# Layer norm behind attention on VectorE: three runs of four tiles, or eight steps of one or two tiles between the bias steps

## The chip, the cores and the metric

The kernel runs on one core of a Trainium2 chip. The metric is the device time of one execution in microseconds (us), the median of several runs.

## The reference

The whole program is one transformer block: adaptive layer norm, attention with a relative bias, a gated residual, a second adaptive layer norm, and a mixture of eight experts (top 2) with a gated residual. There are 8 batches of 512 tokens, 256 channels and 16 heads of width 16.

```python
mod = (_silu(L0_c) @ L0_wmod).reshape(L0_c.shape[0], 6, 1, -1)
sa, ca, ga, sb, cb, gb = ...
h = _layernorm(x, axis=-1) * (1 + ca) + sa
x = x + ga * _L0_attn_ref(h, W_qkv, b_qkv, W_out, b_out, rel_bias)
h = _layernorm(x, axis=-1) * (1 + cb) + sb      # the layer norm of this study
x = x + gb * _L0_ffn_ref(h, gate_w, expert_bias, w_up, w_down)
```

The second layer norm takes the mean and the variance of each token's 256 channels of the gated attention result, subtracts the mean, divides by the root of the variance plus 1e-5, and scales and shifts by rows of the batch.

## The kernel before

**Stages.** Four parts follow one another: preparation, attention (from about 88 us to 845 us of the profiled execution), routing, and experts. Only attention is touched.

**Attention.** An outer loop goes over the 8 batches, an inner one over the 16 heads n of a batch. The first and the last batch are written out, the six between them are one loop body (`Fori`). All engines run their own instruction streams, in the order of the code, and meet at semaphores. One head is one step. TensorE (PE) makes the scores of 4 tiles of 128 queries by 512 keys (L888, two buffers in PSUM), turns the exponentials of the head before, in two pairs of tiles (L897), and weighs the values of the head before that (L912). VectorE (DVE) adds the bias to each score tile and takes its minimum (`add_bias`, L761, four a step, t from 0 to 3), and moves the first pair of turned tiles out of PSUM (`evacuate`, L769). ScalarE (ACT) takes the exponentials (L683) and moves the second pair (L690). The tile t of `sn` is written again one head later, when its exponential is taken.

**The shared bank.** One PSUM bank, `ps_m`, serves in turn for the small products of a batch: the table `USES` gives each its step. Those of the steps 9, 10, 12 and 13 project q1, k1, v0 and v1 for the next batch ("project steps"; some 1.9 us of PE); "back1" at step 11 turns one group of outputs back, which VectorE divides (L783, L785); VectorE adds the bias of v (`values`, L776) behind v0 and v1.

**The layer norm.** During batch b the results of batch b-1 are finished. On VectorE, `between(b, n, kind)` is called twice a step: with n between bias tile 1 and `evacuate`, and with n + 0.5 between bias tile 3 and bias tile 0 of the next step. At 9.5 stands `moments` (four BN_STATS, L806, then four BN_AGGR, L812), at 10.5 `centre` (four SCALAR_TENSOR_TENSOR, L819: minus the mean, times the scale row), at 12.5 `normal` (four of the same kind, L828: times 1/deviation, plus the shift row). Each works on tiles of 128x256 in SBUF.

**GpSimd (POOL)** runs, in this order, in the middle of a batch: the split of q1 into bf16 parts (`split`: L417, L419, L423, L425), `deviation` (L618, L620; waits for `mv_done`, all four BN_AGGR), `split_piece` 2 of the experts' weights (L578, L580), the split of k1 (the same four lines), `split_piece` 3, `move_v` (L568, waits for `values` of v1), and `rest_of` (L606, L610; waits for `h2_done`, all four of `normal`). In the last batch there is nothing to project or to split of q and k.

**Behind it.** PE turns the normalised rows (L959) at the steps 14 and 14.5, after `h2_done`. SyncE stores them, and loads the stacks of q and k for the next batch (L445) when the last scores are made.

Of the kernel before, what the change touches and what calls it, by code (L numbers as in the profile page):

```python
# [16 lines left out]
B, S, D = 8, 512, 256  # L17
# [5 lines left out]
TB = S // P  # L23
# [16 lines left out]
def at_least(engine, semaphore, value):  # L40

    if not isinstance(value, int) or value > 0:
        engine.wait_ge(semaphore, value)


def apart(engine, passed):

    engine.sem_inc(passed, 1)
# [259 lines left out]
        (15.5, "logits"))  # L308
FROM_BEFORE = ("back3", "turn0", "turn1", "out0", "out1", "rows0", "rows1", "logits")
FOR_NEXT = ("q0", "k0", "q1", "k1", "v0", "v1")  # L310
MOMENTS, CENTRED, NORMAL = 9.5, 10.5, 12.5


def attention(nc, ahead, logits, x, h1t, mod_rows, ext_rows, splits, w_up_t, w_down_t, w_parts, rest_rows, h2_rows, sums):
# [10 lines left out]
    with ExitStack() as ctx:  # L325
# [59 lines left out]
        def uses_of(kind):  # L385

            return [(n, u) for n, u in USES
                    if not (kind == "first" and u in FROM_BEFORE) and not (kind == "last" and u in FOR_NEXT)]
# [5 lines left out]
        def use(b, kind, name):  # L394

            return uses_before(b, kind) + [u for _, u in uses_of(kind)].index(name)

        def end_use(name):

            return uses_before(B - 1, "last") + len(uses_of("last")) + FROM_BEFORE.index(name)  # L400
# [344 lines left out]
        def _(dve):  # L745
# [25 lines left out]
            def values(b, j, at):  # L771

                dve.wait_ge(used, at + 1)

                at_least(dve, v_moved, b * 2)
                dve.tensor_tensor(v_next[:, 2 * j:2 * j + 2, :], ps_m[:, :].rearrange("p (t n) -> p t n", n=D),  # L776
                                  b_v[:, :].unsqueeze(1).to_broadcast([P, 2, D]), ALU.add).then_inc(freed, 1)

            def back(b, g, at):

                dve.wait_ge(used, at + 1)
                turned_back = ps_m[:, :].rearrange("p (h t w) -> p h t w", h=TB, t=TB)
                dve.reciprocal(inv[:, :, :], turned_back[:, :, :, DK]).then_inc(inv_done, 1)  # L783
                dve.wait_ge(inv_done, b * GROUPS + g + 1)
                dve.tensor_tensor(on[:, :, g * TB * DK:(g + 1) * TB * DK].rearrange("p t (h d) -> p h t d", d=DK),  # L785
                                  turned_back[:, :, :, 0:DK], inv[:, :, :].unsqueeze(3).to_broadcast([P, TB, TB, DK]),
                                  ALU.mult).then_inc(freed, 1)

            def gate_out(b, j, at):

                dve.wait_ge(used, at + 1)
                dve.wait_ge(x_in, b * 48 + 48)

                at_least(dve, rest_out, b * 16)
                dve.wait_ge(sums_zeroed, 16 * (B + 1))
                dve.tensor_tensor(gated[:, 2 * j:2 * j + 2, :], ps_m[:, :].rearrange("p (t n) -> p t n", n=D),
                                  ga[:, :].unsqueeze(1).to_broadcast([P, 2, D]), ALU.mult).then_inc(freed, 1)

                dve.wait_ge(freed, at + 1)
                dve.sem_inc(gated_done, 1)  # L800

            def moments(b):

                dve.wait_ge(x1_done, b * 2 + 2)
                for t in range(TB):
                    dve.bn_stats(stats[:, t, :], gated[:, t, :]).then_inc(stats_done, 1)  # L806

                at_least(dve, rstd_done, b)
                dve.wait_ge(stats_done, (b + 1) * TB)
                apart(dve, dve_passed)  # L810
                for t in range(TB):
                    dve.bn_aggr(mv[:, t, :], stats[:, t, :]).then_inc(mv_done, 1)  # L812

            def centre(b):

                dve.wait_ge(mv_done, (b + 1) * TB)
                apart(dve, dve_passed)
                for t in range(TB):
                    dve.scalar_tensor_tensor(out=xb[:, t, :], in0=gated[:, t, :], scalar=mv[:, t, 0:1], in1=mod2[:, D:2 * D],  # L819
                                             op0=ALU.subtract, op1=ALU.mult).then_inc(centred, 1)  # L820

            def normal(b):

                dve.wait_ge(rstd_done, b + 1)
                dve.wait_ge(centred, (b + 1) * TB)
                apart(dve, dve_passed)
                for t in range(TB):
                    dve.scalar_tensor_tensor(out=xb[:, t, :], in0=xb[:, t, :], scalar=rstd[:, t:t + 1], in1=mod2[:, 0:D],  # L828
                                             op0=ALU.mult, op1=ALU.add).then_inc(h2_done, 1)

            def keep_logits(b, at):
                dve.wait_ge(used, at + 1)
                dve.tensor_copy(logits[:, bass.ds(b * TB, TB), :],
                                ps_m[:, 0:TB * NE].rearrange("p (t e) -> p t e", e=NE)).then_inc(freed, 1)

            def between(b, n, kind):
                for m, u in uses_of(kind):
                    if m == n and u == "back3":
                        back(b - 1, 3, use(b, kind, u))
                    elif m == n and u[:4] == "back":  # L840
                        back(b, int(u[4]), use(b, kind, u))
                    elif m == n and u[:3] == "out":
                        gate_out(b - 1, int(u[3]), use(b, kind, u))
                    elif m == n and u[0] == "v":
                        values(b + 1, int(u[1]), use(b, kind, u))
                    elif m == n and u == "logits":
                        keep_logits(b - 1, use(b, kind, u))
                if kind != "first" and n == MOMENTS:
                    moments(b - 1)
                if kind != "first" and n == CENTRED:  # L850
                    centre(b - 1)
                if kind != "first" and n == NORMAL:
                    normal(b - 1)

            for j in range(2):
                values(0, j, 4 + j)
# [1 line left out]
            def batch(b, kind):  # L858
                for n in range(NH):
                    if kind == "first" and n % TB == 0:  # L860
                        dve.wait_ge(ahead.loaded[n // TB], 16 * TB)
                    add_bias(b, n, 0)
                    add_bias(b, n, 1)
                    between(b, n, kind)
                    if kind != "first" or n > 0:
                        evacuate(b * NH + n - 1, (n + 1) % 2)
                    add_bias(b, n, 2)
                    add_bias(b, n, 3)
                    between(b, n + 0.5, kind)
# [3 lines left out]
            back(B - 1, 3, end_use("back3"))  # L873
            for j in range(2):
                gate_out(B - 1, j, end_use(f"out{j}"))
            moments(B - 1)
            centre(B - 1)
            normal(B - 1)
            keep_logits(B - 1, end_use("logits"))

        @block.tensor
# [823 lines left out]
```

## Time and profile before

| | us |
|---|---|
| median of 3 runs | 1387.36 (1382.64 to 1391.23) |
| profiled execution, its own time | 1386.03 |
| its span, first to last instruction | 1384.4 |
| busy in the span: PE / DVE / ACT / POOL | 1148.3 / 918.4 / 670.2 / 693.5 |

The profiled execution is 1.33 us below the median and 1.63 us above its own span. The busy times are sums over stages with different limits, so they say little about one step of attention; for that the rows below show the instructions in order of time. A start of the copy L769 marks the same point of each step, and the distance between two of them is the length of a step.

### The profile page before, as it was taken

To read this page: it belongs to the slowest core of one execution; us is meant where nothing else is said; L and a number is where in the kernel's file an instruction comes from. 1 tells how busy PE (TensorE), PEld (TensorE's weight loads), DVE (VectorE), ACT (ScalarE), POOL (GpSimd) and SP (SyncE) were. 2 spreads that over 40 slices of the span, in tenths; PEclk is the share of its full clock that TensorE was granted. 3 is DMA by queue.
4 is the path that set the end of the run, shared out by engine and by line. 5 is a ranking of instruction groups with operands and counts; after the bars stand their busy time and mean duration, and the time that the engine had idled before them with its cause. 6 is when DMAs were issued, how large, how long until landed. Compare 5 with 4: busy or idle time off the path is not lost. (4 is left out here: it accounts for less than half of the span.)

```text
span 1384.4 us, 33297 instructions
## 1 busy us (share of the span) xinstructions
PE 1148.3 (83%) x11290; PEld 898.9 (65%) x11291; DVE 918.4 (66%) x2185; ACT 670.2 (48%) x1038; POOL 693.5 (50%) x715
## 2 busy tenths in 40 slices
PE   5469999898998998998999861399999999999910
PEld 3236776676766766766777541288888888888810
DVE  4547888687786885885888846655555555555556
ACT  4248776675765766765768630222222222222212
POOL 3215155354551543463433332857666766666656
PEclk9779999999898998998999995599999999999965
DMA  9596853663556356526636117114342443442354
GB/s 308 182 208 185 238 165 92 151 130 95 152 104 146 124 110 144 119 81 151 130 79 163 47 52 262 47 38 109 47 109 44 112 106 61 95 106 46 46 153 129
DMA packets 123137, 168.47 MB, mean 122 GB/s; under 512 B 13016, under 2 KB 99288, under 8 KB 123008
## 3 DMA queue, kind: packets, MB, share of 16 engines
q1 hardware_dynamic: 103136, 137.59, 37.4%
q0 software_dynamic: 19872, 29.15, 11.2%
q8 instruction: 82, 1.34, 0.4%
q14 instruction: 47, 0.39, 0.1%
HBM read 105.74 MB, written 60.96 MB: 120 GB/s over the span
## 5 line engine op out<-in xcount | busy, mean ns | idle before, releaser
L683 ACT ACTIVATE b_pr<-b_sn,b_mn 128x512 f32<-128x512 f32 x512 | 341.9, 717 | 132.6 <-DVE b_mn L761 128.6
L761 DVE CUSTOM_DVE_ANT_0 b_sn<-b_ps_s,s_tile 128x512 f32<-128x512 f32 x512 | 332.5, 686 | 90.9 <-PE b_ps_s L888 41.6
L897 PE MATMUL b_ps_t<-b_ident,b_pr 128*128 128x128 f32 x2048 | 280.5, 282 | 8.6 <-ACT b_pr L683 7.4
L897 PEld LDWEIGHTS b_ps_t<-b_ident,b_pr 128*128 128x128 f32 x2048 | 245.6, 145 | 54.2 <-ACT b_pr L683 21.1
L1492 ACT ACTIVATE d_g<-d_ps_u 128x512 f32<-128x512 f32 x156 | 92.9, 599 | 317.0 <-PE d_ps_u L1605 221.5
L888 PE MATMUL b_ps_s<-b_ks,b_qs 96*128 96x512 bf16 x512 | 195.4, 404 | 55.3 <-DVE b_mn L761 27.6
L1605 PE MATMUL d_ps_u<-d_xp,k_wu 128*128 128x256 bf16 x1776 | 201.5, 274 | 0.0
L1620 PE MATMUL d_ps_y<-k_wd,d_gp 128*128 128x256 bf16 x1776 | 199.9, 273 | 0.0
L769 DVE COPY b_pt<-b_ps_t 128x1024 f32<-128x1024 f32 x128 | 156.5, 1223 | 53.8 <-PE b_ps_t L897 49.9
L1605 PEld LDWEIGHTS d_ps_u<-d_xp,k_wu 128*128 128x128 bf16 x1776 | 173.5, 98 | 21.7 <-issue 0.3
L1620 PEld LDWEIGHTS d_ps_y<-k_wd,d_gp 128*128 128x128 bf16 x1776 | 173.8, 98 | 20.1
L690 ACT ACTIVATE b_pt<-b_ps_t 128x1024 f32<-128x1024 f32 x128 | 131.3, 1026 | 106.9 <-PE b_ps_t L897 106.2
L1444 POOL DMA_INDIRECT sums<-d_yo,d_places x78 | 129.4, 1659 | 57.6 <-issue 25.9
L912 PE MATMUL b_ps_o<-b_pt,b_v 128*32 128x128 f32 x4096 | 146.7, 287 | 0.2 <-ACT b_pt L690 0.2
L912 PEld LDWEIGHTS b_ps_o<-b_pt,b_v 128*32 128x32 f32 x4096 | 110.0, 114 | 45.0 <-issue 42.7
L1530 DVE CAST d_xp<-d_ps_x 128x512 bf16<-128x512 f32 x39 | 27.0, 692 | 143.5 <-PE d_ps_x L1592 97.0
L888 PEld LDWEIGHTS b_ps_s<-b_ks,b_qs 96*128 96x128 bf16 x512 | 49.1, 99 | 110.5 <-DVE b_mn L761 67.6
L1544 DVE TENSOR_TENSOR d_gp<-d_g,d_gp 128x512 bf16<-128x512 f32 x156 | 109.0, 698 | 5.4
L1542 DVE CAST d_gp<-d_g 128x512 bf16<-128x512 f32 x156 | 69.5, 446 | 59.9 <-ACT d_g L1492 43.5
L1421 POOL DMA_INDIRECT d_xg<-h_rows,d_tokens x80 | 80.8, 1010 | 47.3 <-POOL d_tokens L1417 33.8
L1433 POOL DMA_INDIRECT d_gates<-gate_rows,d_places x78 | 79.6, 1020 | 43.3 <-POOL d_places L1429 22.2
L587 POOL TENSOR_TENSOR b_gab<-b_ga,s_b_o 128x256 f32<-128x256 f32 x8 | 5.8, 723 | 164.0 <-DMA b_mod<-mod_rows 164.0
(192 smaller groups left out, 1254.3 us busy)
## 6 DMA issues: line engine op xcount, KB each, us to landing
w_parts<-b_w_split SPq DMA_DIRECT2D x32, 512.0 KB, 3.4
splits<-b_parts SPq DMA_DIRECT2D x32, 384.0 KB, 2.6
b_qs<-splits SPq DMA_DIRECT2D x96, 128.0 KB, 4.8
b_ks<-splits SPq DMA_DIRECT2D x96, 128.0 KB, 6.9
b_w_raw<-in_w_up_t SPq DMA_DIRECT2D x16, 512.0 KB, 8.7
b_w_raw<-in_w_down_t SPq DMA_DIRECT2D x16, 512.0 KB, 6.1
k_wu<-w_parts SPq DMA_DIRECT2D x8, 1024.0 KB
k_wd<-w_parts SPq DMA_DIRECT2D x8, 1024.0 KB
```

The source lines that it names most:

```text
L683: act.activation(pr[:, m, t, :], sn[:, t, :], ACT.Exp, bias=mn[:, m, t:t + 1], scale=-1.0).then_inc(exped, 1)
L690: act.activation(pt[:, m, 2:4, :], ps_t[:, 2:4, :], ACT.Copy).then_inc(out_act, 1)
L761: dve.tensor_tensor_reduce(sn[:, t, :], ps_s[:, t % 2, :], ahead.tile[:, n, at:at + S], -1.0, BIG, ALU.add, ALU.min, mn[:, n % 2, t:t + 1] ...
L769: dve.tensor_copy(pt[:, m, 0:2, :], ps_t[:, 0:2, :]).then_inc(out_dve, 1)
L888: pe.matmul(ps_s[:, t % 2, :], qs[:, half, m, t * P:(t + 1) * P], ks[:, half, m, :], start=True, stop=True).then_inc(scored, 1)
L897: mm = pe.transpose(ps_t[:, j, t * P:(t + 1) * P], pr[:, m, t, j * P:(j + 1) * P], ident[:, :])
L912: mm = pe.matmul(ps_o[2 * DK * t:2 * DK * (t + 1), n % TB * P:(n % TB + 1) * P], v[:, j, n, :], pt[:, n % 2, j, t * P:(t + 1) * P], start= ...
L1444: pool.indirect_dma_start(sums, bass.IndirectOffsetOnAxis(ap=places[:, u, 0, i:i + 1], axis=0), yo[:, u, i, :], None, compute_op=ALU.add). ...
L1492: act.activation(g[:, j, :], ps_u[:, j, :], ACT.Gelu).then_inc(gelued, 1)
L1544: dve.tensor_tensor(gp[:, u, 1, at], g[:, j, :], gp[:, u, 0, at], ALU.subtract).then_inc(g_split, 1)
L1605: mm = pe.matmul(ps_u[:, j // 2, j % 2 * ROWS:(j % 2 + 1) * ROWS], kept.wu[:, slot, w, c, j * P:(j + 1) * P], xp[:, u, x, c * ROWS:(c + 1) ...
L1620: mm = pe.matmul(ps_y[:, i, 0:D], gp[:, u, x, j * ROWS + i * P:j * ROWS + (i + 1) * P], kept.wd[:, slot, w, j, :], start=(j == 0 and n == ...
```

## The change

`moments` is cut into the statistics of the tiles 0 and 1 (at 9.5) and 2 and 3 (at 10), and a new `collect` (the four BN_AGGR, at 10.5). `centre` takes tile 0 at 11, tiles 1 and 2 at 11.5, tile 3 at 12. `normal` takes tiles 0 and 1 at 12.5 and tiles 2 and 3 at 13. Operations, shapes and their number stay; the waits are those of before, one set for each piece. Behind the last batch all stands as it did.

```diff
-            def moments(b):
+            def moments(b, ts):
 
                 dve.wait_ge(x1_done, b * 2 + 2)
-                for t in range(TB):
+                for t in ts:
                     dve.bn_stats(stats[:, t, :], gated[:, t, :]).then_inc(stats_done, 1)
+
+            def collect(b):
 
                 at_least(dve, rstd_done, b)
                 dve.wait_ge(stats_done, (b + 1) * TB)
...
-            def centre(b):
+            def centre(b, ts):
 
                 dve.wait_ge(mv_done, (b + 1) * TB)
                 apart(dve, dve_passed)
-                for t in range(TB):
+                for t in ts:
...
-            def normal(b):
+            def normal(b, ts):
 
                 dve.wait_ge(rstd_done, b + 1)
                 dve.wait_ge(centred, (b + 1) * TB)
                 apart(dve, dve_passed)
-                for t in range(TB):
+                for t in ts:
...
-                if kind != "first" and n == MOMENTS:
-                    moments(b - 1)
-                if kind != "first" and n == CENTRED:
-                    centre(b - 1)
-                if kind != "first" and n == NORMAL:
-                    normal(b - 1)
+                if kind == "first":
+                    return
+                if n == 9.5:
+                    moments(b - 1, (0, 1))
+                if n == 10:
+                    moments(b - 1, (2, 3))
+                if n == 10.5:
+                    collect(b - 1)
+                if n == 11:
+                    centre(b - 1, (0,))
+                if n == 11.5:
+                    centre(b - 1, (1, 2))
+                if n == 12:
+                    centre(b - 1, (3,))
+                if n == 12.5:
+                    normal(b - 1, (0, 1))
+                if n == 13:
+                    normal(b - 1, (2, 3))
```

The order of instructions on PE, ScalarE, GpSimd and SyncE is the same in both kernels. On VectorE it changes between the steps 9 and 13. Line numbers are one lower after the change up to L806 (L761 is L760, L806 is L805) and one higher from L812 on (L813, L820, L829). An `ISA` row with two operands is a bias tile, and the `ISA b_mn` behind it reads its minimum.

VectorE in the loop body, from the end of bias tile 3 of step 10 to the bias tiles of step 11, before:

```order
L761 ISA b_sn,b_mn<-b_ps_s,s_tile 128x512
L761 ISA b_mn 128x1
L819 SCALAR_TENSOR_TENSOR b_xb<-b_gated,b_mv,b_mod 128x256 x4
L756 ISA
L43 REGISTER_ALU
L761 ISA b_sn,b_mn<-b_ps_s,s_tile 128x512
L761 ISA b_mn 128x1
L756 REGISTER_ALU
L43 REGISTER_ALU
L761 ISA b_sn,b_mn<-b_ps_s,s_tile 128x512
L761 ISA b_mn 128x1
```

and after:

```order
L760 ISA b_sn,b_mn<-b_ps_s,s_tile 128x512
L760 ISA b_mn 128x1
L813 BN_AGGR b_mv<-b_stats 128x2 x4
L755 ISA
L43 REGISTER_ALU
L760 ISA b_sn,b_mn<-b_ps_s,s_tile 128x512
L760 ISA b_mn 128x1
L755 REGISTER_ALU
L43 REGISTER_ALU
L760 ISA b_sn,b_mn<-b_ps_s,s_tile 128x512
L760 ISA b_mn 128x1
```

The four tiles of `centre` stood between the last bias tile of step 10 and the first of step 11; the four small BN_AGGR now stand there.

VectorE from the division of back1 (step 11) on, before:

```order
L785 TENSOR_TENSOR b_on<-b_ps_m,b_inv 128x4x4x16
L766 ISA
L769 COPY b_pt<-b_ps_t 128x1024
L756 REGISTER_ALU
L43 REGISTER_ALU
L761 ISA b_sn,b_mn<-b_ps_s,s_tile 128x512
L761 ISA b_mn 128x1
L756 REGISTER_ALU
L761 ISA b_sn,b_mn<-b_ps_s,s_tile 128x512
```

and after:

```order
L784 TENSOR_TENSOR b_on<-b_ps_m,b_inv 128x4x4x16
L820 SCALAR_TENSOR_TENSOR b_xb<-b_gated,b_mv,b_mod 128x256
L765 ISA
L768 COPY b_pt<-b_ps_t 128x1024
L755 REGISTER_ALU
L43 REGISTER_ALU
L760 ISA b_sn,b_mn<-b_ps_s,s_tile 128x512
L760 ISA b_mn 128x1
L755 REGISTER_ALU
L760 ISA b_sn,b_mn<-b_ps_s,s_tile 128x512
L760 ISA b_mn 128x1
L820 SCALAR_TENSOR_TENSOR b_xb<-b_gated,b_mv,b_mod 128x256 x2
```

Tile 0 of `centre` now stands between the division and the copy of step 11, and tiles 1 and 2 stand between the bias tiles 3 of step 11 and 0 of step 12.

VectorE from `values` of v0 (step 12) on, before:

```order
L776 TENSOR_TENSOR b_v_next<-b_ps_m,s_b_v 128x512
L766 ISA
L769 COPY b_pt<-b_ps_t 128x1024
L756 REGISTER_ALU
L43 REGISTER_ALU
L761 ISA b_sn,b_mn<-b_ps_s,s_tile 128x512
L761 ISA b_mn 128x1
L756 REGISTER_ALU
L761 ISA b_sn,b_mn<-b_ps_s,s_tile 128x512
L761 ISA b_mn 128x1
L828 SCALAR_TENSOR_TENSOR b_xb<-b_xb,b_rstd,b_mod 128x256 x4
```

and after:

```order
L775 TENSOR_TENSOR b_v_next<-b_ps_m,s_b_v 128x512
L820 SCALAR_TENSOR_TENSOR b_xb<-b_gated,b_mv,b_mod 128x256
L765 ISA
L768 COPY b_pt<-b_ps_t 128x1024
L755 REGISTER_ALU
L43 REGISTER_ALU
L760 ISA b_sn,b_mn<-b_ps_s,s_tile 128x512
L760 ISA b_mn 128x1
L755 REGISTER_ALU
L760 ISA b_sn,b_mn<-b_ps_s,s_tile 128x512
L760 ISA b_mn 128x1
L829 SCALAR_TENSOR_TENSOR b_xb<-b_xb,b_rstd,b_mod 128x256 x2
```

Tile 3 of `centre` has come between `values` and the copy of step 12, and two tiles of `normal` are left at 12.5; the other two stand behind `values` of v1, ahead of the copy of step 13.

## Rows read from the trace of the kernel before

**Rows 1.** Stretches, batch 3: length, busy PE, PEld, DVE, ACT, POOL; PEclk, DMA share, GB/s.

```profile
403.20:411.10 7.90, 5.45 (x65) 4.18 (x64) 7.87 (x17) 4.62 (x8) 7.36 (x7) 1.00 0.09 29
411.10:417.30 6.20, 6.20 (x55) 4.44 (x54) 4.50 (x12) 3.96 (x6) 3.17 (x2) 0.73 0.48 175
```

**Rows 2.** Timeline of DVE, batch 0, copies of steps 10 to 13: start, length.

```profile
134.05 1.23 DVE L769 COPY b_pt<-b_ps_t 128x1024 f32<-128x1024 f32 x1 [1.38 <-PE b_ps_t L897]
...
138.73 1.22 DVE L769 COPY b_pt<-b_ps_t 128x1024 f32<-128x1024 f32 x1
...
144.25 1.23 DVE L769 COPY b_pt<-b_ps_t 128x1024 f32<-128x1024 f32 x1 [0.18 <-PE b_ps_t L897]
...
149.78 1.22 DVE L769 COPY b_pt<-b_ps_t 128x1024 f32<-128x1024 f32 x1 [0.18 <-PE b_ps_t L897]
```

**Rows 3.** Timeline of DVE, batch 3, from the copy of step 9 to that of 14.

```profile
397.58 1.23 DVE L769 COPY b_pt<-b_ps_t 128x1024 f32<-128x1024 f32 x1 [1.47 <-PE b_ps_t L897]
...
399.94 1.40 DVE L806 BATCH_NORM_STATS2 b_stats<-b_gated 128x6 f32<-128x256 f32 x4
...
401.47 0.38 DVE L812 BATCH_NORM_AGGREGATE b_mv<-b_stats 128x2 f32<-128x6 f32 x4
...
403.15 1.22 DVE L769 COPY b_pt<-b_ps_t 128x1024 f32<-128x1024 f32 x1
...
405.51 3.84 DVE L819 SCALAR_TENSOR_TENSOR b_xb<-b_gated,b_mv,b_mod 128x256 f32<-128x256 f32 x4
...
409.27 0.68 DVE L761 CUSTOM_DVE_ANT_0 b_sn<-b_ps_s,s_tile 128x512 f32<-128x512 f32 x1
...
410.49 0.25 DVE L783 RECIPROCAL b_inv<-b_ps_m 128x16 f32<-128x16 f32 x1
...
411.12 1.22 DVE L769 COPY b_pt<-b_ps_t 128x1024 f32<-128x1024 f32 x1
...
417.26 1.23 DVE L769 COPY b_pt<-b_ps_t 128x1024 f32<-128x1024 f32 x1
...
419.61 1.67 DVE L828 SCALAR_TENSOR_TENSOR b_xb<-b_xb,b_rstd,b_mod 128x256 f32<-128x256 f32 x4
...
423.02 1.22 DVE L769 COPY b_pt<-b_ps_t 128x1024 f32<-128x1024 f32 x1
...
427.40 1.23 DVE L769 COPY b_pt<-b_ps_t 128x1024 f32<-128x1024 f32 x1 [0.37 <-PE b_ps_t L897]
```

**Rows 4.** Timeline of POOL, batch 3, the same stretch.

```profile
402.36 1.05 POOL L620 TENSOR_TENSOR b_rstd<-b_rstd,b_power 128x4 f32<-128x4 f32 x1
...
404.49 2.15 POOL L580 TENSOR_TENSOR b_w_split<-b_w_raw,b_w_split 128x1024 bf16<-128x1024 f32 x1
...
406.57 0.81 POOL L417 CAST b_parts<-b_qf 128x512 bf16<-128x512 f32 x1
...
407.46 1.21 POOL L419 TENSOR_TENSOR b_rest<-b_qf,b_parts 128x512 f32<-128x512 f32 x1
...
408.94 0.88 POOL L423 CAST b_parts<-b_rest 128x512 bf16<-128x512 f32 x1 [0.27 <-POOL b_rest L419]
...
409.90 1.17 POOL L425 TENSOR_TENSOR b_parts<-b_rest,b_parts 128x512 bf16<-128x512 f32 x1
...
411.26 1.04 POOL L578 CAST b_w_split<-b_w_raw 128x1024 bf16<-128x1024 f32 x1 [0.19 <-POOL b_parts L425]
...
423.36 0.61 POOL L568 COPY b_v<-b_v_next 128x512 f32<-128x512 f32 x1 [8.84 <-DVE b_v_next L776]
```

**Rows 5.** Timeline of PE, batch 3, a score of step 11.

```profile
410.02 0.39 PE L888 MATMUL b_ps_s<-b_ks,b_qs 96*128 96x512 bf16 x1 [2.15 <-DVE b_mn L761]
```

**Rows 6.** Timeline of DVE, last batch, copies of the steps 9 and 14.

```profile
767.95 1.23 DVE L769 COPY b_pt<-b_ps_t 128x1024 f32<-128x1024 f32 x1 [0.39 <-PE b_ps_t L897]
...
797.81 1.23 DVE L769 COPY b_pt<-b_ps_t 128x1024 f32<-128x1024 f32 x1 [0.51 <-PE b_ps_t L897]
```

**Rows 7.** Timeline of DVE, first bias tile behind the loop's jump back.

```profile
444.09 0.69 DVE L761 CUSTOM_DVE_ANT_0 b_sn<-b_ps_s,s_tile 128x512 f32<-128x512 f32 x1 [6.73 <-issue]
```

More of the change, by code:

```diff
@@ L310 @@
 FOR_NEXT = ("q0", "k0", "q1", "k1", "v0", "v1")
-MOMENTS, CENTRED, NORMAL = 9.5, 10.5, 12.5
 def attention(nc, ahead, logits, x, h1t, mod_rows, ext_rows, splits, w_up_t, w_down_t, w_parts, rest_rows, h2_rows, sums):
@@ L875, in _ @@
                 gate_out(B - 1, j, end_use(f"out{j}"))
-            moments(B - 1)
-            centre(B - 1)
-            normal(B - 1)
+            moments(B - 1, range(TB))
+            collect(B - 1)
+            centre(B - 1, range(TB))
+            normal(B - 1, range(TB))
             keep_logits(B - 1, end_use("logits"))
```

## The prediction

> **What bounds the kernel now.** I read first the timeline of VectorE by the copy L769, which marks one point of each step. Batch 0 has no layer norm; its steps 10, 11 and 12, from copy to copy, take 4.68, 5.52 and 5.53 us [rows 2]. The same steps of batch 3 take 7.97, 6.14 and 5.76 us [rows 3]. The step with `centre` in front of its bias tiles is 3.29 us longer, the next 0.62, the one with `normal` 0.23; step 9, with `moments`, takes 5.57. From the copy of step 9 to that of step 14 batch 3 needs 29.82 us [rows 3]. So four tiles of arithmetic in one run are the main loss, and `moments` and `normal` cost little where they stand: they fit into VectorE's idle time in project steps, like the 1.38 us ahead of the copy of step 10 in batch 0 [rows 2].
>
> Two more views say why `centre` is so dear. In the stretch of step 10 VectorE is busy 7.87 of 7.90 us and PE 5.45 [rows 1]: VectorE is the bound there. But four tiles of `normal` take 1.67 us and four of `centre`, the same operation and size, take 3.84 [rows 3]. Side by side with GpSimd's timeline the reason shows: L580 runs to 406.64, and `centre`, issued at 405.51, goes on only then; GpSimd's next cast L417 takes 0.81 instead of some 0.6, and L423 0.88 [rows 4]. The two engines take turns: a `centre` tile that finds a GpSimd operation running waits until that ends, then needs about 0.28 us more to its own end; the GpSimd operation waiting behind it ends about its own length less 0.15 us after. Undisturbed a tile takes 0.40 us of VectorE (1.67 by four), and the bias tiles and the copy are not held. The third view, of PE, has the consequence: the score of step 11 came 2.15 us late [rows 5], and in the stretch behind it the granted clock is 0.73 of full speed [rows 1], a mixture of the two levels 2.4 and 1.2 GHz. That is most of the 0.62 us of step 11.
>
> **The change, in a walk.** No instruction on data is added or taken away: eight pieces in place of three runs, with more waits that are long fulfilled. Their own cost I bound by 0 below and, above, by 0.07 us each, what lies between the end of L812 and the next bias tile beyond the normal pitch (my estimate from rows 3); in idle time it is 0, and I take 0. What counts is where each piece meets GpSimd, whose order is the same. I count from the copy of step 9 (397.58 = 0) and use: copy and two bias tiles 2.36 (397.58 to 399.94), two bias tiles 1.22 (409.27 to 410.49), the division 0.63 (410.49 to 411.12) [rows 3], and 0.61 for `values`, which has the size of a bias tile.
>
> Statistics. Two BN_STATS are 0.70 (half of 1.40), once at 2.36 and once at 4.28. They end at 5.0. PE's pair of transposes for the copy of step 10 ends at 5.53 as in batch 0, so the copy starts there (5.57 before): worth 0.04 us. BN_STATS is not held by GpSimd: the four took 1.40 while GpSimd was busy with the q1 split.
>
> `collect` and GpSimd. The four BN_AGGR run from 7.89 to 8.27 (0.38, [rows 3]) in the idle time ahead of bias tile 0, at no cost. But `mv_done` now comes at 8.27, where it came at 4.27 (401.85). GpSimd's `deviation` waits for it, and behind it in the same queue stand `split_piece` 2, the split of k1 and `split_piece` 3, all 4.0 us later. Who waits for these: the store of the k1 parts and the weight pieces, with the load of the stacks only at the end of the batch, and `move_v`, where GpSimd waits 8.84 us for VectorE anyway [rows 4]. So the delay itself is hidden. What it moves is the turns: L620 ends at 9.83, L578 runs to 10.84, L580 to 13.10, L417 of k1 to 13.64, and so on (lengths from [rows 4]).
>
> Step 10. The copy of step 11 would start at 5.53 + 4.68 = 10.21 (batch 0). There `centre` tile 0 is issued, finds L578, and ends at 10.84 + 0.28 = 11.12; the copy starts 0.08 before that end, 11.04. Before it was 13.54: **2.50 us won**.
>
> Step 11. Bias tile 3 ends at 13.40. Tile 1 finds L417 and ends at 13.92; L419 takes its turn and ends at 14.94; tile 2 ends at 15.22. The bias tiles then end at 16.36, `values` at 16.97. GpSimd's L425 has ended at 16.93 and its L578 starts only at 17.12 (it starts 0.19 behind L425 [rows 4]), so tile 3 goes free, 0.40, and the copy of step 12 starts at 17.37. The step takes 6.33, where batch 0 has 5.52 and before 6.14. The PE waits in it are 0.65 and 0.2 us, far from 2.15, so I leave the clock at full speed.
>
> Step 12. Bias tile 3 ends at 19.73. GpSimd's L580 (pushed a little by tile 3) ends at 20.56, so the first `normal` ends at 20.84, the second leaves VectorE at 21.16; bias tiles 22.38, `values` of v1 22.99. GpSimd's `move_v` starts 0.34 us behind that (423.36 against the copy at 423.02, [rows 3, 4]), so of the two `normal` tiles now at 13 the first is free and the second waits for L568 (0.61): the copy of step 13 starts at 24.12. Step 12 takes 6.75 against 5.76: **1.0 lost**.
>
> Step 13. VectorE is now late, and the way copy, bias tiles, exponentials, transposes, copy takes 4.38 us (423.02 to 427.40 [rows 3]). End: 28.50 in place of 29.82. **1.32 us a batch**, times 6 batches of the loop: 7.9 us.
>
> `h2_done` comes at 24.2, later than before in the batch (23.7); PE's turn of the rows in step 14 comes after 26 and does not wait.
>
> Last batch. Steps 9 to 13 take 29.86 us [rows 6]. Without projections there is less idle time. By the same walk: copies at 0, 4.94 (the second pair of statistics no longer fits), 10.44 (tile 0 behind L578), 17.55 (tile 1 behind a cast L578, tile 2 behind L580, which is 2.15 long), 22.8, 27.2. It wins 2.6 us; I take 2.4, since a late score there can cost some clock. Behind the last batch nothing changes.
>
> Sum: 1386.03 - 7.9 - 2.4 = **1375.7 us** for the profiled execution, 0.8% under the median of 1387.36, which lies 1.33 above that execution. I forecast 1376. A difference under 1% is about what a measurement of this kernel can't tell from no change.
>
> **A rule beside the rows.** The walk rests on who goes first. The rows show turns: L417 was next in GpSimd's queue at 406.57 and still was stretched to 0.81 by the waiting `centre` tile [rows 4]. The Trainium skill, "SBUF — State Buffer", section "Who interferes with whom", says that a VectorE instruction with two inputs in SBUF and a GpSimd instruction that reads SBUF exclude each other, and that whichever is issued first holds the port for its whole length; one with a single SBUF input is not concerned. The rows agree for `centre`, for BN_STATS and for the bias tiles (one input in PSUM). The rule speaks against the change in one respect: a run of four pays the first wait once, while pieces can each meet a fresh long operation. By its worst reading every one of the eight tiles waits out an L580: that sum is the bound of the third rival.
>
> **The rivals.** (a) *The turns cost nothing.* If the pieces find GpSimd between operations, as `normal` does before, each tile is 0.40. The walk then gives copies at 5.53, 10.61, 16.29, 22.24 and 26.62: 3.2 us a batch, 19.2 in six, 5.3 in the last, **1361.5 us**. For it: the walk has margins of a few tenths. Against: GpSimd's queue from 8.46 to 20.5 has hardly a gap.
>
> (b) *Nothing is left over.* Tile 3 misses its gap of 0.15 us and waits out L578: the copy of step 12 is 1.0 us later. That makes L580 later too, which then is passed before `normal`, and gives back some 0.6. Also 0.07 for each of five more waits on the path: the gain is about 0.6 a batch, 3.6 + 2.0: **1380 us**.
>
> (c) *Slower, by the clock.* PE's waits in the steps 11 and 12 could lower its granted clock twice a batch instead of once. Which is the case is decided by the length of PE's gap: 2.15 us was followed by the lower level [rows 5, 1]; the walk has 0.65 and 0.5. The gaps reach 2 us if two tiles of a piece each wait out an L580 (2.15, [rows 4]). A step with the clock at 0.73 and no layer norm in it cost 0.62; in it about half of the time ran at the lower level, so a project step wholly at that level costs about twice as much, by my estimate 1.3. Two of them turn the 1.32 won into 1.3 lost a batch, and with rival (b) into about 2: 6 x 1.6 - 2 = some 7 us more, **1393 us**. The Trainium skill, "TensorE: Matmul & The Clock Gate", tells the same direction, that an array which has idled runs at half clock; the price here is from the rows.
>
> (d) *The jump back.* Behind the loop's end VectorE waits 6.73 us for no engine [rows 7]; it is longer by a few instructions now, and this wait may move by a microsecond either way per pass, without sign. It widens every case by some 3 us.
>
> **How the numbers follow.** The walk's own case 0.5 (1371 to 1379), (a) or half of it 0.25 (1361 to 1371), (b) 0.18 (1379 to 1386), (c) 0.07. The likeliest is 1376. For 8 in 10, I leave out (c) and the outer part of (a): 1366 to 1386. Faster by over 1% is below 1373.5: (a) and a quarter of the walk's case, 0.37. Slower by over 1% is above 1401.2, which needs more than (c): 0.04. The rest, 0.59, is within 1%.
>
> **What would show it.** In the changed profile: the copies of the steps 10 to 14 at 5.5, 11.0, 17.4, 24.1 and 28.5 us behind that of step 9; the single `centre` tile about 0.9 us long, of the two one near 0.55 and one near 1.3; L618 about 4 us later against the copy of step 9; granted clock 1.00 in step 11; the mean of L820 still well over 0.48 us. The forecast is wrong if GpSimd's operations don't hold the pieces (then much faster), or if PE's score rows in the steps 11 or 12 show waits near 2 us and a clock below 1 (then slower), or if the stretch at the jump back differs by more than a microsecond.

## The result, and the profile after

| us | before | changed |
|---|---|---|
| median of 10 runs | 1385.53 (1380.39 to 1391.23) | 1379.12 (1374.50 to 1382.55) |
| profiled execution | 1386.03 | 1376.14 |
| its span | 1384.4 | 1374.5 |

The ratio is 0.995, 95% interval 0.993 to 0.9971: the change makes the kernel faster by half a percent. A second set of 11 runs gave 1377.39 against 1384.10, ratio 0.9958 (0.994 to 0.9975).

VectorE's timeline of batch 3 in the changed kernel, which answers to [rows 3] (start, length, and in brackets the idle time ahead):

```profile
400.03 1.23 DVE L768 COPY b_pt<-b_ps_t 128x1024 f32<-128x1024 f32 x1 [1.46 <-PE b_ps_t L911]
...
402.39 0.75 DVE L805 BATCH_NORM_STATS2 b_stats<-b_gated 128x6 f32<-128x256 f32 x2
...
404.26 0.75 DVE L805 BATCH_NORM_STATS2 b_stats<-b_gated 128x6 f32<-128x256 f32 x2
405.59 1.23 DVE L768 COPY b_pt<-b_ps_t 128x1024 f32<-128x1024 f32 x1 [0.58 <-PE b_ps_t L911]
...
407.95 0.38 DVE L813 BATCH_NORM_AGGREGATE b_mv<-b_stats 128x2 f32<-128x6 f32 x4
...
410.33 0.82 DVE L820 SCALAR_TENSOR_TENSOR b_xb<-b_gated,b_mv,b_mod 128x256 f32<-128x256 f32 x1
411.08 1.21 DVE L768 COPY b_pt<-b_ps_t 128x1024 f32<-128x1024 f32 x1
...
413.43 1.86 DVE L820 SCALAR_TENSOR_TENSOR b_xb<-b_gated,b_mv,b_mod 128x256 f32<-128x256 f32 x2
...
417.04 0.47 DVE L820 SCALAR_TENSOR_TENSOR b_xb<-b_gated,b_mv,b_mod 128x256 f32<-128x256 f32 x1
417.43 1.21 DVE L768 COPY b_pt<-b_ps_t 128x1024 f32<-128x1024 f32 x1
...
419.78 1.51 DVE L829 SCALAR_TENSOR_TENSOR b_xb<-b_xb,b_rstd,b_mod 128x256 f32<-128x256 f32 x2
...
423.04 1.22 DVE L829 SCALAR_TENSOR_TENSOR b_xb<-b_xb,b_rstd,b_mod 128x256 f32<-128x256 f32 x2
424.18 1.21 DVE L768 COPY b_pt<-b_ps_t 128x1024 f32<-128x1024 f32 x1
...
428.55 1.22 DVE L768 COPY b_pt<-b_ps_t 128x1024 f32<-128x1024 f32 x1 [0.52 <-PE b_ps_t L911]
```

The copies of the steps 10 to 14 stand 5.56, 11.05, 17.40, 24.15 and 28.52 us behind that of step 9; the walk gave 5.53, 11.04, 17.37, 24.12 and 28.50. Before they stood at 5.57, 13.54, 19.68, 25.44 and 29.82 [rows 3]. Where nothing holds them, one tile lasts 0.47 us and two last 0.87 (the kernel early_collect below has both, in its last batch). Here four of the pieces are longer: the single `centre` tile 0 lasts 0.82 us, tiles 1 and 2 together 1.86, the two of `normal` at 12.5 1.51 and those at 13 1.22. Only tile 3 of `centre` has its 0.47.

GpSimd's timeline beside it, answering to [rows 4]:

```profile
408.52 0.23 POOL L617 TENSOR_SCALAR b_rstd<-b_mv 128x4 f32<-128x4 f32 x1 [4.48 <-DVE b_mv L813]
...
409.85 1.03 POOL L577 CAST b_w_split<-b_w_raw 128x1024 bf16<-128x1024 f32 x1
410.95 2.20 POOL L579 TENSOR_TENSOR b_w_split<-b_w_raw,b_w_split 128x1024 bf16<-128x1024 f32 x1
413.10 0.61 POOL L416 CAST b_parts<-b_qf 128x512 bf16<-128x512 f32 x1
413.79 1.22 POOL L418 TENSOR_TENSOR b_rest<-b_qf,b_parts 128x512 f32<-128x512 f32 x1
...
417.32 1.08 POOL L577 CAST b_w_split<-b_w_raw 128x1024 bf16<-128x1024 f32 x1 [0.19 <-POOL b_parts L424]
418.48 2.13 POOL L579 TENSOR_TENSOR b_w_split<-b_w_raw,b_w_split 128x1024 bf16<-128x1024 f32 x1
423.36 0.61 POOL L567 COPY b_v<-b_v_next 128x512 f32<-128x512 f32 x1 [2.75 <-DVE b_v_next L775]
```

L617 waited 4.48 us for the BN_AGGR (L813). Its queue then runs from 408.52 to 420.6, through the pieces of `centre` and the first of `normal`. The cast L577 starts at 417.32, 0.28 us behind the start of `centre` tile 3 at 417.04: the gap that the walk had found was there in five of the six batches of the loop. In the first of the six GpSimd's k1 split was 0.2 us later, tile 3 met its last operation (L424) and lasted 0.59, and the copy of step 14 came at 28.73.

PE's late scores of the steps 11 and 12 (answering to [rows 5]), and the stretches of these two steps (columns as in [rows 1]):

```profile
412.96 0.39 PE L902 MATMUL b_ps_s<-b_ks,b_qs 96*128 96x512 bf16 x1 [0.56 <-DVE b_mn L760]
...
419.30 0.39 PE L902 MATMUL b_ps_s<-b_ks,b_qs 96*128 96x512 bf16 x1 [0.38 <-DVE b_mn L760]
```

```profile
411.08:417.43 6.35, 5.57 (x61) 4.37 (x60) 6.35 (x15) 3.70 (x5) 5.73 (x6) 1.00 0.01 3
417.43:424.18 6.75, 6.14 (x64) 4.54 (x62) 6.75 (x16) 3.80 (x6) 3.71 (x3) 1.00 0.56 207
```

These gaps are 0.56 and 0.38 us where one was 2.15, and the granted clock is 1.00 in both stretches, where a stretch of 6.20 us had 0.73 [rows 1]. The last batch is another matter. There tiles 1 and 2 wait out a cast and an L579 (3.25 us for the two), and a score of step 11 comes 1.94 us late:

```profile
774.83 0.39 PE L902 MATMUL b_ps_s<-b_ks,b_qs 96*128 96x512 bf16 x1 [1.94 <-DVE b_mn L760]
```

Behind it, in step 12, the granted clock is 0.67.

### The profile page after: what moved, and what is told of

Read it like the earlier page. It is cut to its first block and busy times, and to the rows that moved or that the text cites. A ratio compares the mean times of both kernels' runs of the same rounds, so it can differ in the third digit from the quotient of the medians.

```text
span 1374.5 us, 33318 instructions
## 1 busy us (share of the span) xinstructions
PE 1140.6 (83%) x11290; PEld 894.3 (65%) x11291; DVE 916.4 (67%) x2185; ACT 668.7 (49%) x1038; POOL 691.1 (50%) x715
## 3 DMA queue, kind: packets, MB, share of 16 engines
q0 software_dynamic: 19872, 29.15, 11.3%
## 5 line engine op out<-in xcount | busy, mean ns | idle before, releaser
L760 DVE CUSTOM_DVE_ANT_0 b_sn<-b_ps_s,s_tile 128x512 f32<-128x512 f32 x512 | 331.9, 685 | 80.6 <-PE b_ps_s L902 37.0
L911 PE MATMUL b_ps_t<-b_ident,b_pr 128*128 128x128 f32 x2048 | 277.4, 280 | 7.1 <-ACT b_pr L682 5.5
L768 DVE COPY b_pt<-b_ps_t 128x1024 f32<-128x1024 f32 x128 | 156.3, 1221 | 57.9 <-PE b_ps_t L911 54.5
L926 PE MATMUL b_ps_o<-b_pt,b_v 128*32 128x128 f32 x4096 | 141.7, 280 | 0.2 <-ACT b_pt L689 0.2
L926 PEld LDWEIGHTS b_ps_o<-b_pt,b_v 128*32 128x32 f32 x4096 | 106.4, 111 | 42.0 <-issue 41.4
```

Source lines behind the costliest of these rows:

```text
L760: dve.tensor_tensor_reduce(sn[:, t, :], ps_s[:, t % 2, :], ahead.tile[:, n, at:at + S], -1.0, BIG, ALU.add, ALU.min, mn[:, n % 2, t:t + 1] ...
L768: dve.tensor_copy(pt[:, m, 0:2, :], ps_t[:, 0:2, :]).then_inc(out_dve, 1)
L911: mm = pe.transpose(ps_t[:, j, t * P:(t + 1) * P], pr[:, m, t, j * P:(j + 1) * P], ident[:, :])
L926: mm = pe.matmul(ps_o[2 * DK * t:2 * DK * (t + 1), n % TB * P:(n % TB + 1) * P], v[:, j, n, :], pt[:, n % 2, j, t * P:(t + 1) * P], start= ...
```

## The experiments

All positions are the copy L769 (L768 in most kernels here, L770 or L771 in some) in us behind the copy of step 9, batch 3. They stand for the loop's batches within 0.1 us unless said otherwise, the first of the six excepted, which is up to 0.25 us longer in the kernels with a part of the change in them. "Last" is step 14 of the last batch. The ratio is to the kernel before, run beside it on the same chip: on the chip of stats_only and runs_pool_waits its median was 1386.61, beside the others 1384.10 to 1385.53.

| kernel | step 11 | 12 | 13 | 14 | last | median us | ratio (95%) |
|---|---|---|---|---|---|---|---|
| before | 13.54 | 19.68 | 25.44 | 29.82 | 29.86 | 1385.53 | |
| changed | 11.05 | 17.40 | 24.15 | 28.52 | 27.16 | 1379.12 | 0.995 (0.993-0.9971) |
| early_collect | 11.04 | 18.89 | 25.33 | 29.70 | 24.55 | 1383.48 | 0.998 (0.9959-1.0002) |
| normal_run | 11.05 | 17.40 | 23.80 | 28.17 | 27.07 | 1374.38 | 0.9896 (0.9855-0.9938) |
| centre_run | 11.90 | 17.46 | 24.20 | 28.57 | 25.11 | 1371.39 (one run) | |
| stats_only | 11.91 | 17.47 | 23.85 | 28.22 | 25.12 | 1370.76 | 0.9891 (0.9858-0.9925) |
| after_light_pool | 10.69 | 16.48 | 22.92 | 27.29 | 24.05 | 1366.42 | 0.9866 (0.9838-0.9894) |
| before_light_pool | 11.36 | 16.93 | 22.69 | 27.07 | 25.12 | 1363.28 | 0.9855 (0.9829-0.988) |
| pool_moved | 11.37 | 17.15 | 22.91 | 27.28 | 24.54 | 1365.95 | 0.9854 (0.982-0.9889) |
| before_pool_moved | 13.53 | 21.00 | 26.76 | 31.14 | 26.21 | 1380.67 | 0.9971 (0.9946-0.9996) |
| runs_pool_waits | 11.36 | 16.92 | 22.69 | 27.07 | 25.13 | 1368.64 | 0.9863 (0.9834-0.9891) |

### Where do the statistics stand: early_collect

```diff
-                if n == 9.5:
-                    moments(b - 1, (0, 1))
-                if n == 10:
-                    moments(b - 1, (2, 3))
-                if n == 10.5:
-                    collect(b - 1)
+                if n == 9.5:
+                    moments(b - 1, range(TB))
+                    collect(b - 1)
```

> The changed kernel with all of the statistics and BN_AGGR back at 9.5, centre and normal in pieces as changed. Theory 1 (turns with GpSimd decide): mv_done comes at 4.3 us behind the copy of step 9 again, GpSimd's weight piece 3 (L578, L580) then meets the two centre tiles at 11.5, the second of which waits out an L580. Copies of the steps 10 to 14 at 5.57, 11.05, 18.8, 25.2 and 29.6 us behind that of step 9: 1.0 us a batch worse than the changed kernel (28.5), nearly the time of before (29.8); total some 6 us above the changed kernel. Rival 2 (only the length of a run between bias tiles counts, GpSimd does not): the statistics fit in the idle time at 9.5 as they did before, so 28.5 stays, within 0.2.

The copy of step 14 came at 29.70 (29.6 expected). The two `centre` tiles at 11.5, on VectorE and then GpSimd's rows:

```profile
413.40 3.36 DVE L820 SCALAR_TENSOR_TENSOR b_xb<-b_gated,b_mv,b_mod 128x256 f32<-128x256 f32 x2
```

```profile
404.47 0.23 POOL L617 TENSOR_SCALAR b_rstd<-b_mv 128x4 f32<-128x4 f32 x1 [0.46 <-DVE b_mv L813]
...
413.17 1.04 POOL L577 CAST b_w_split<-b_w_raw 128x1024 bf16<-128x1024 f32 x1 [0.19 <-POOL b_parts L424]
414.28 2.19 POOL L579 TENSOR_TENSOR b_w_split<-b_w_raw,b_w_split 128x1024 bf16<-128x1024 f32 x1
```

3.36 us for two tiles, against 1.86: the first waited out the cast L577, the second the L579 behind it. With `mv_done` 4 us earlier GpSimd is elsewhere in its queue. So the cutting of `centre` and `normal` alone is worth 0.1 us a batch against this profile of the kernel before, and is a loss of 0.5 against its batches in which the clock did not fall (29.23, below); GpSimd counts. In the last batch, which I had not worked out, the same placing helps, 24.55 against 27.16: there the weight pieces run ahead of `centre`. So the median lies 4 us above that of the changed kernel and not 6.

### Is a cut normal worth anything: normal_run

```diff
                 if n == 12.5:
-                    normal(b - 1, (0, 1))
-                if n == 13:
-                    normal(b - 1, (2, 3))
+                    normal(b - 1, range(TB))
```

> The changed kernel with the four tiles of normal back in one run at 12.5. Theory 1: the first tile waits out L580 as now, the other three are 0.40 each, and no tile meets move_v's copy: copy of step 13 at 23.8 in place of 24.1, that of step 14 at 28.2: 0.3 us a batch better, 2 us in all. Rival 2 (shorter runs are always better): 0.2 to 0.8 worse a batch. Last batch: 0.1 to 0.3 worse or better, no sign claimed.

Copy of step 13 at 23.80, of 14 at 28.17, as expected: this part of the change costs 0.35 us a batch. In the last batch it costs 0.1 us (27.07 against 27.16).

### Is a cut centre worth anything: centre_run and stats_only

```diff
-                if n == 11:
-                    centre(b - 1, (0,))
-                if n == 11.5:
-                    centre(b - 1, (1, 2))
-                if n == 12:
-                    centre(b - 1, (3,))
+                if n == 10.5:
+                    centre(b - 1, range(TB))
```

stats_only has this and the edit of normal_run.

> The changed kernel with centre back in one run of four at 10.5, behind collect; statistics and normal in pieces as changed. Theory 1: centre is the piece whose spreading pays. The four tiles alternate with L618, L620 and L578: copy of step 11 near 13.5, step 11 near 6.1 with a lowered clock, copy of step 13 near 26.0, of step 14 near 30.4: 0.5 us worse than before (29.8), since normal's spreading alone costs. Rival: spreading the statistics or normal carries the gain: 29.3 or less.

My theory missed by 1.8 us: 28.57 in place of 30.4. VectorE, then GpSimd:

```profile
402.48 1.22 DVE L768 COPY b_pt<-b_ps_t 128x1024 f32<-128x1024 f32 x1 [0.58 <-PE b_ps_t L907]
...
404.84 0.37 DVE L813 BATCH_NORM_AGGREGATE b_mv<-b_stats 128x2 f32<-128x6 f32 x4
405.37 1.69 DVE L820 SCALAR_TENSOR_TENSOR b_xb<-b_gated,b_mv,b_mod 128x256 f32<-128x256 f32 x4 [0.15 <-DVE b_mv L813]
...
408.82 1.22 DVE L768 COPY b_pt<-b_ps_t 128x1024 f32<-128x1024 f32 x1
```

```profile
405.40 0.23 POOL L617 TENSOR_SCALAR b_rstd<-b_mv 128x4 f32<-128x4 f32 x1 [4.46 <-DVE b_mv L813]
405.71 1.06 POOL L619 TENSOR_TENSOR b_rstd<-b_rstd,b_power 128x4 f32<-128x4 f32 x1
406.75 1.20 POOL L577 CAST b_w_split<-b_w_raw 128x1024 bf16<-128x1024 f32 x1
```

The four tiles in one run lasted 1.69 us, free. Right behind the BN_AGGR GpSimd has only L617 and L619 to do, on 128x4; they ran beside the tiles and held none of them visibly, though L619 also reads two operands. (The other way round a hold is seen: in the last batch of centre_run and of stats_only L617 lasts 0.50 us in place of 0.23.) I had let them alternate as the large ones do. The first large operation, L577, came at 406.75, when the run was nearly over, and was itself stretched to 1.20. So the late `mv_done` opens a door: while GpSimd waits for it and finishes its two small operations, `centre` runs. The rival of that entry, that spreading the other parts carries the gain, is not proved by 28.57; stats_only asks:

> Of the change only the statistics' part: BN_STATS at 9.5 and 10, collect at 10.5, then centre in one run of four at 10.5 and normal in one run of four at 12.5, as before. Theory 1, as centre_run amended it (what pays is that the late mv_done keeps GpSimd waiting while centre runs; cutting centre and normal is worth nothing): copies of the steps 11, 12, 13 and 14 at 11.9, 17.5, 23.8 and 28.2 us behind that of step 9, 0.3 under the changed kernel; total 1373 to 1377. Rival (the pieces of centre or normal carry part of the gain): 28.6 or more.

28.22 and 25.12, median 1370.76 (2 us under the range expected, whose upper end is inside the interval of the ratio): with the statistics' part alone the kernel is 1.1% under before, where the whole change gives 0.5%. Added to the late statistics, the cut `centre` gives nothing in the loop (28.52 against 28.57 in centre_run) and costs 2 us in the last batch, and the cut `normal` costs 0.35 a batch.

### The price of the turns: after_light_pool and before_light_pool

```diff
-                pool.tensor_copy(w_split[:, i, 0, :], w_raw[:, i, :]).then_inc(w_high, 1)
+                w = slice(0, 8) if n >= 2 else slice(0, WC)
+                pool.tensor_copy(w_split[:, i, 0, w], w_raw[:, i, w]).then_inc(w_high, 1)
...
+            w = slice(0, 8) if passed is not None and k == 3 else slice(0, S)
-            engine.tensor_copy(out[:, 0, :], qf[:, k % 2, :]).then_inc(split_step, 1)
+            engine.tensor_copy(out[:, 0, w], qf[:, k % 2, w]).then_inc(split_step, 1)
```

(and so on in the other lines of the two functions)

> The changed kernel in which GpSimd leaves out most of the work of the weight pieces 2 and 3 and of the k1 split (8 columns in place of 1024 and 512; the output is therefore not the reference's). With before_light_pool it prices GpSimd's turns. Theory 1: copies of the steps 10 to 14 near 5.5, 10.7, 16.4, 22.3 and 26.8, a tile of centre 0.47: 1.7 us a batch under the changed kernel. Rival 2 (GpSimd doesn't matter): 28.5 stays.

> The kernel before with the same GpSimd work left out. Theory 1: four centre tiles take 1.7 us in place of 3.84, the clock does not fall: copy of step 11 near 11.4, of step 14 near 27.1, so 2.7 us a batch under before; against after_light_pool only 0.3 to 0.5 a batch remain as the worth of spreading itself. Rival 2: 29.8 stays, or the difference to after_light_pool is still 1.3 or more.

Without the large operations the changed kernel needs 27.29, 1.23 less (1.7 expected), and the kernel before 27.07, 2.75 less. The order turns round: with nobody to wait for, the three runs of before are 0.2 us a batch better in the loop than the eight pieces. I had expected them 0.3 to 0.5 worse. The positions say which pieces lose. At the copy of step 12, with `centre` done, the pieces are ahead, 16.48 against 16.93: the run of `centre` lengthens step 10 to 5.79, 1.1 over batch 0's, and the pieces cost 0.7 in two steps. Then step 12 takes 6.44 us with two `normal` tiles ahead of the copy of step 13, and 5.76 with all four in one run at 12.5. In the last batch the pieces are 1.1 us better (24.05 against 25.12), so over seven batches the two orders are equal, 187.8 and 187.5 us for the steps 9 to 13.

### GpSimd moved instead: pool_moved, before_pool_moved, runs_pool_waits

```diff
+                split_piece(b, 2)
                 for k in range(2, 4):
...
                     if k == 2 and kind != "first":
                         deviation(b - 1)
+                        pool.wait_ge(centred, b * TB)
-                    split_piece(b, k)
                 if kind != "last":
                     move_v(b + 1, 0, use(b, kind, "v1") + 1)
+                split_piece(b, 3)
```

The wait for `centred` is in runs_pool_waits alone. That and before_pool_moved have VectorE's order of before; pool_moved has the `centre` pieces of the change, statistics at 9.5 and `normal` in one run.

> GpSimd's two weight pieces are moved out of the way: piece 2 ahead of the q1 split (GpSimd idles 4.6 us there), piece 3 behind move_v; statistics back at 9.5, centre in pieces at 11, 11.5 and 12, normal in one run at 12.5. Theory 1: only centre tile 0 meets an operation (L425, some 0.9 us longer); copies of the steps 10 to 14 at 5.57, 11.2, 16.8, 22.6 and 27.0 us: 2.8 us a batch under before, 1.5 under the changed kernel; in the last batch 5 under before. Total 1364 to 1368. Rival 2 (GpSimd doesn't matter): 28 to 28.5, like the changed kernel. Rival 3 (the time at the loop's jump back takes up what the steps give): steps shorter as said, the total not under 1375.

> The kernel before with GpSimd's order of pool_moved alone. Theory 1: the run of four centre tiles at 10.5 (issued at 7.9) now meets L419, L423 and L425 of the k1 split in place of L580, L417 and L419; copy of step 11 at 13.4 (before 13.54), copy of step 14 at 29.7: within 0.3 us a batch of before, total unchanged within 3 us. Rival: moving the weight pieces is what helps by itself: 1 us or more a batch.

> VectorE's order exactly as in the kernel before; only GpSimd changes: weight piece 2 ahead of the q1 split, the k1 split behind a wait for the four centre tiles, piece 3 behind move_v. Theory 1: no centre tile meets a GpSimd operation, four take 1.7 us; copies of the steps 10 to 14 at 5.58, 11.4, 16.9, 22.7 and 27.07 us, as in before_light_pool; last batch near 25.1 or less. 2.75 us a batch and 4.7 in the last under before: 1362 to 1367. Rival (one run of four tiles is itself too long): 29 or more.

pool_moved came to 27.28 (27.0 expected) and to 1365.95. before_pool_moved shows how much hangs on the meeting: its six batches took 27.25, 29.23, 31.14, 29.23, 29.23 and 29.81 us for the steps 9 to 13. Step 10, with the run of four `centre` tiles, is 5.97 us in the first and 7.95 in the others. In the first, weight piece 2 waited for its DMA, the k1 split came later, and the run of four met little of it. In the third VectorE waits 1.76 us for a score in step 11. PE's rows there say why: the score of step 11 that comes 2.14 us late already takes 0.61 us in place of 0.39, and the transposes behind it 1.91 in place of the 1.04 of the batch before:

```profile
404.88 0.61 PE L889 MATMUL b_ps_s<-b_ks,b_qs 96*128 96x512 bf16 x1 [2.14 <-DVE b_mn L762]
405.28 1.91 PE L898 MATMUL b_ps_t<-b_ident,b_pr 128*128 128x128 f32 x8
```

The granted clock of this step 11 is 0.66, a fall that began before the late score; in the sixth batch it is 0.72, and in the other four 1.00. I had expected every batch within 0.3 us of before; the median, 0.3% under before, is near what was expected. With the wait added (`centre`, then GpSimd with the k1 split behind it):

```profile
402.98 1.67 DVE L821 SCALAR_TENSOR_TENSOR b_xb<-b_gated,b_mv,b_mod 128x256 f32<-128x256 f32 x4
```

```profile
390.55 1.04 POOL L578 CAST b_w_split<-b_w_raw 128x1024 bf16<-128x1024 f32 x1
...
404.92 0.61 POOL L417 CAST b_parts<-b_qf 128x512 bf16<-128x512 f32 x1 [4.05 <-DVE b_xb L821]
```

the four tiles take 1.67 us in one run and every batch but the first of the six 27.07 (28.14 there). 1368.64 against 1386.61 on its chip (1362 to 1367 expected). VectorE's order is that of before, so one run was not too long; what it met was. In that first batch GpSimd was late by a weight piece that waited for its DMA, and the run met it.

### The missing microseconds: after_again, before_again, before_padded

The steps 9 to 13 sum, over seven batches, to 208.9 us before and 198.5 after, 10.4 apart where the walk said 10.3, and yet the medians are 6.4 apart.

> The changed kernel unaltered, for the jump back. The first two medians differ by 6.4 us and the walk gives 10.5. Theory A (chance): the step with the jump back and the step behind it, summed over five passes (92.7 us before, 90.2 after in the two profiles), spread by some 3 us from one execution to the next with no tie to the change; here anywhere from 88 to 96, and the steps 9 to 13 again 28.5. Theory B (the gain is partly given back there): the sum is 94 or more, above all profiles of kernels with the old VectorE order.

> The kernel before unaltered, for a second profile and as the measure of chance: steps 9 to 13 29.8 us a batch again; the ratio to itself within 0.2% of 1. If chance rules the jumps, their sum of five passes lies elsewhere than 92.7 by 1 us or more, and the part from the last batch's step 15 to the end of the span moves by 1 us or more from 581.1.

> The kernel before with three more semaphore instructions a batch on VectorE (at 10, 11.5 and 13), as many more as the changed kernel executes; no wait is added. It asks whether the 4 us by which the medians moved less than the walk come from the longer instruction stream. Theory C (length of the stream or its alignment costs at the jumps and behind attention): 1387 to 1389 median, the five passes of the jump with the step behind it sum to 94 or more. Theory A (chance, or where in time the pass falls): 1384 to 1386, sum as in the kernel before, 88 to 93.

before_padded differs from before by this:

```diff
+                if kind != "first" and n in (10, 11.5, 13):
+                    apart(dve, dve_passed)
```

| | steps 9-13, seven batches | jumps, five | behind step 15 | median, ratio (95%) |
|---|---|---|---|---|
| before | 208.9 | 92.7 | 581.1 | |
| before_again | 206.7 | 88.1 | 583.0 | 1387.51, 1.0011 (0.9991-1.003) |
| before_padded | 207.3 | 87.8 | 583.2 | 1387.04, 1.0003 (0.9981-1.0024) |
| changed | 198.5 | 90.2 | 583.6 | |
| after_again | 199.8 | 92.5 | 582.3 | 1377.39, 0.9958 (0.994-0.9975) |

("Jumps" is from the copy of step 15 to that of step 1 of the next batch; "behind step 15" from the last batch's copy to the end of the span.) The longer stream costs nothing that is seen: the median, 1387.04, lies in the range given for theory C, but the kernel before had 1386.61 on that chip, and the jumps sum to 87.8, not 94. Chance moves the jumps by 4.9 us between three profiles with VectorE's old order, and over all fourteen profiles they lie between 87.8 and 95.3, the end part between 580.8 and 586.5. And the steps themselves are not fixed in the kernel before, which I had taken for granted: PE in batch 3 of before_again, the late score, and the stretch of step 11 behind it:

```profile
413.79 0.39 PE L888 MATMUL b_ps_s<-b_ks,b_qs 96*128 96x512 bf16 x1 [2.16 <-DVE b_mn L761]
```

```profile
414.88:420.45 5.57, 4.86 (x54) 3.59 (x52) 4.44 (x12) 3.90 (x6) 3.17 (x2) 1.00 0.42 151
```

The same gap as in [rows 5], 2.16 us, and no fall of the clock: 1.00, and the step takes 5.57 in place of 6.14. Of the loop's six batches two escaped it in before_again and one in before_padded, and the last batch gained 0.7 both times. So the profile that I read was the dearest of three, 1.6 to 2.2 us of its loss being a clock that does not always fall. With before_pool_moved there are 23 batches of the loop with such a gap (2.14 to 2.18 us), and the clock fell in or just ahead of step 11 in 17. In the changed kernel the same chance stands in the last batch, behind its gap of 1.94 us; step 12 in its two profiles:

```profile
775.71:780.96 5.25, 5.25 (x53) 3.79 (x52) 5.24 (x14) 4.01 (x6) 0.00 (x0) 0.67 0.35 135
```

```profile
777.01:783.53 6.52, 6.52 (x57) 4.86 (x56) 5.34 (x15) 3.98 (x6) 0.00 (x0) 0.61 0.29 110
```

5.25 us in one, 6.52 in the other, where the lower clock began already in step 11 (0.88 over that step, 1.00 in the first profile). The steps then save 6.9 to 10.4 us, by which profiles are paired. Theory B, that the jumps take back a part, is left open by these five (89.5 us on average in the three profiles of before and its padded twin, 91.4 in the two of the changed kernel, with a spread of 5). All fourteen profiles lean to it: the six with VectorE's order of before have 87.8 to 92.7 us, 89.5 on average, the eight with a part of the change in it 90.2 to 95.3, 92.0 on average. That is 2.5 us, with overlap, and about what is missing; what would cause it is not shown.

## Why the prediction was right, and what it got wrong

The forecast was 1376, range 1366 to 1386, "within 1%" at 0.59; measured 1379.12. The mechanism and the sizes in the loop are shown; the total is off by 3 us, because a gain of 10.3 was forecast and the medians moved by 6.4.

- *The walk through a batch.* All five positions of the loop were right within 0.03 us, and the last batch's 27.2 measured 27.16. This last is in part luck: the second profile of the same kernel has 28.41, by the clock. The assumption behind it, turns with GpSimd at the price of its whole operation, is shown by early_collect (29.70), normal_run (28.17) and the two light kernels. Its limit is centre_run, where I let L618 and L620 alternate with the tiles and they held none.
- *Step 12 loses 1.0 us.* Right: it takes 6.75 us as in the walk. The cut of `normal` is 0.35 of it, by normal_run.
- *`collect` later moves GpSimd by 4.0 us, hidden.* Right as to the delay (L617 starts 8.49 us behind the copy of step 9, L618 before at 4.46). But I booked it as a shift of the turns only. It is the one part of the change that gains in the loop: stats_only 28.22 against 28.52 with all parts.
- *"So four tiles of arithmetic in one run are the main loss".* Wrong, and wrong against my own next paragraph. In before_light_pool and runs_pool_waits the run stands where it was and the batch takes 27.07. Of the 4.05 us that batch 3 takes over batch 0 (29.82 against 25.77, copies at 128.53 and 154.30), 2.75 were the turns and the clock behind them.
- *Rival (a), no turns: 3.2 us a batch.* The pieces without the large operations gave 27.29 where 26.62 was worked out; most of the difference is step 12, where I let the copy of step 13 go at 22.24.
- *The sum, 7.9 us for six batches and 2.4 for the last.* Measured 10.4 in the profiles at hand, so the sum was right for them. What it had wrong is its starting point: it takes every batch of the kernel before at the 29.82 us of one profile, and with that the clock's fall behind the 2.15 us gap as certain. Two more profiles of the same order show 206.7 and 207.3 in place of 208.9; by them and the changed kernel's 198.5 and 199.8 the gain is 6.9 to 8.8. The medians' 6.4 and 6.7 leave up to 2 us for the jumps and the end part, which is not settled. That the profiles agree with the sum to 0.1 us is thus luck, and the 2.4 for the last batch is 0.7 or 0.8 if the second profiles are paired (29.17 and 29.15 against 28.41).
- *Rival (b)* did not occur: tile 3 never met L578. *Rival (c)* did not occur in the loop: gaps of 0.56 and 0.38, clock 1.00. In the last batch it did, once: two tiles waited out a cast and an L579, the gap was 1.94 us, and the clock was 0.67 or 0.61 in step 12. But its sentence that the length of PE's gap decides is wrong: gaps of the same 2.14 to 2.18 us were followed by a lowered clock and by a full one. *Rival (d)*: the wait at the jump moves as said, about 5 us over five passes, and not by the stream's length.
- *The SBUF rule of the Trainium skill.* The Trainium skill, "SBUF — State Buffer", section "Who interferes with whom", has a VectorE operation with two SBUF inputs contend with a GpSimd operation that reads SBUF, and the one issued later block until the other ends. The trace agrees for 128x512 and larger (3.36 us for two tiles in early_collect); for L617 and L619 (128x4) no hold of a tile is seen in centre_run, where four tiles took 1.69 us beside them.

## What to carry to other kernels

Before an operation is cut up or moved because it is "too long", compare its time with that of the same operation elsewhere in the trace: 3.84 against 1.67 us for four tiles said that it was waiting, and the queue to mend was the other engine's. Two-input SBUF work on VectorE belongs where GpSimd is waiting for VectorE itself (here behind the operation that releases it, or ahead of a wait set for it); that gave 1.1% by moving the statistics alone, and 1.4% with VectorE untouched. And price a lowered PE clock from more than one profile: behind the same gap it was lowered in six batches of six in one and, for all or part of a step, in four of six in another.

## What was not expected of the hardware

- A PE gap of 2.15 us is followed by a granted clock of 0.73 in one profile (before) and one of 2.16 us by 1.00 in another (before_again), same kernel, same step.
- Small GpSimd operations (128x4, one of them 1.06 us long with two operands) did not visibly hold VectorE's two-input tiles (four in 1.69 us, centre_run); large ones held a tile until they ended (two in 3.36 us, early_collect).
- The same loop body can take 27.25 to 31.14 us for the same five steps within one execution (before_pool_moved): by what `centre` met on GpSimd (step 10 5.97 or 7.95 us), and by PE's clock in step 11 (5.57 us at 1.00, 7.47 at 0.66).
